# RWKV block with a routed mixture of experts: two tile lists in place of one, one gap tile a chunk, and the loads of x issued together

## The reference

```python
x = _ln(x, ln0_w, ln0_b)
h = _ln(x, ln1_w, ln1_b)
xx = _time_shift(h)
# xk, xv, xr: h and xx mixed; k, v, sr from three 128x128 matrices
att = _wkv(w, time_first, k, v)          # a scan along each sequence, with a running maximum
x = x + jnp.einsum('btc,oc->bto', sr * att, Wo)
# h2 = _ln(x); kf = relu(Wfk mix)^2; kv = Wfv kf; x + sigmoid(Wfr mix) * kv, then a layernorm
ys = _geglu(xf @ Ws1 + bs1) @ Ws2 + bs2                  # shared expert, all rows
top_val, top_idx = jax.lax.top_k(logits, 2)              # 2 of 12 experts a row
h = jnp.einsum('nd,edh->enh', xf, We1) + be1[:, None, :] # 128 -> 2 * 384, act 384 -> 128
yr = jnp.einsum('end,ne->nd', yE, w)
# layernorm(x + ys + yr)
```

## Time and profile before

| | |
|---|---|
| median of 3 runs | 449.29 us (448.38 to 449.96) |
| the profiled execution | 447.86 us |
| its span, first to last instruction | 446.1 us |
| busy in the span | PE 87%, DVE 70%, ACT 66%, POOL 57% |
| mean granted TensorE clock | 0.967 of full speed |

### The profile page before, as it was taken

The page is one execution under the profiler, slowest core; times in us unless marked ns, Lnnn a source line. Parts: engine busy times, 40 slices in busy tenths (PEclk is TensorE's granted clock), DMA queues, the critical chain, the costliest instruction groups (busy, mean ns, idle before and its releaser), DMA issues.

```text
span 446.1 us, 9927 instructions
## 1 busy us (share of the span) xinstructions
PE 388.3 (87%) x2503; PEld 304.1 (68%) x2503; DVE 311.9 (70%) x1065; ACT 296.4 (66%) x715; POOL 255.8 (57%) x328
## 2 busy tenths in 40 slices
PE   0466799999888997899999599999999999999991
PEld 0224456766665664657444399999999999999840
DVE  3899989999998999763774156666666656665162
ACT  2585689988978775586512177777777777777055
POOL 5676647586647877788777034444444444444273
PEclk9978889999999999999999699999999999999997
DMA  5289910000000300111134577677777677762484
GB/s 156 76 186 314 336 32 0 1 1 2 0 2 31 103 33 7 45 39 44 51 95 160 167 251 248 239 268 251 251 259 251 244 254 253 253 226 103 139 327 119
DMA packets 47247, 64.86 MB, mean 145 GB/s; under 512 B 8796, under 2 KB 31068, under 8 KB 47192
## 3 DMA queue, kind: packets, MB, share of 16 engines
q1 hardware_dynamic: 42744, 54.85, 36.6%
q0 software_dynamic: 4448, 9.38, 6.3%
HBM read 21.65 MB, written 13.91 MB: 80 GB/s over the span
## 4 chain that ended last, share of the span: by engine, by line
PE 57%; DVE 16%; POOL 12%; issue 7%; ACT 5%; DMA 2%; ACTq 0%; DVEq 0%; SPq 0%; POOLq 0%
PE bank L1279 23%; PE bank L1297 11%; POOL dispatched_rows L402 7%; PE bank L986 5%; PE bank L968 3%; DVE rec L554 3%; PE bank L919 2%; PE bank L1271 2%; DVE bst L474 2%; PE bank L920 2%; POOL frs L820 2%; ACT z L689 2%; PE bank L997 2%; PE bank L1330 2%; PE bank L998 2%
## 5 line engine op out<-in xcount | busy, mean ns | idle before, releaser
L1140 POOL DMA_INDIRECT routed_rows<-yo,goes_to x75 | 71.8, 957 | 98.7 <-DVE yo L1189 96.2
L1279 PE MATMUL bank<-xT,w 128*128 128x128 f32 x900 | 114.5, 277 | 0.3 <-issue 0.2
L1279 PEld LDWEIGHTS bank<-xT,w 128*128 128x128 f32 x900 | 108.0, 194 | 0.9 <-issue 0.9
L1181 DVE SCALAR_TENSOR_TENSOR actT<-bank,tile_bias,gl 128x128 f32<-128x128 f32 x225 | 65.2, 345 | 28.0 <-PE bank L1279 22.2
L1233 ACT ACTIVATE gl<-bank,tile_bias 128x128 f32<-128x128 f32 x225 | 66.2, 364 | 14.1 <-PE bank L1279 13.9
L402 POOL DMA_INDIRECT dispatched_rows<-rows_all,slot_i x64 | 64.0, 1000 | 18.6 <-issue 17.4
L1297 PE MATMUL bank<-we_sb,actT 128*128 x450 | 62.7, 275 | 0.9 <-DVE yo L1189 0.9
L1297 PEld LDWEIGHTS bank<-we_sb,actT 128*128 128x128 f32 x450 | 56.1, 192 | 1.2 <-issue 1.1
L1189 DVE SCALAR_TENSOR_TENSOR yo<-bank,goes,wb 128x128 f32<-128x128 f32 x75 | 26.3, 351 | 34.6 <-PE bank L1297 30.0
L1227 ACT ACTIVATE xT<-bank 128x128 f32<-128x128 f32 x75 | 20.8, 277 | 32.2 <-PE bank L1271 31.8
L968 PE MATMUL bank<-xk,wfk_sb 128*128 128x512 f32 x64 | 32.9, 624 | 5.0 <-DVE xk L571 4.5
(11 more groups left out here) (199 smaller groups left out, 761.7 us busy)
## 6 DMA issues: line engine op xcount, KB each, us to landing
w<-we_sb SPq DMA_DIRECT2D x75, 384.0 KB, 3.0
x_all<-dispatched_rows SPq DMA_DIRECT2D x75, 68.0 KB, 1.9
we_sb<-we SPq DMA_DIRECT2D x1, 4608.0 KB
...
routed_rows<-yo,goes_to POOLq DMA_INDIRECT x75
dispatched_rows<-rows_all,slot_i POOLq DMA_INDIRECT x64
```

The lines of the kernel that those rows point to most:

```text
L1140: ng.indirect_dma_start(routed, bass.IndirectOffsetOnAxis(ap=goes_to[n // U % DB][:, n % U:n % U + 1], axis=0), yo[n % YO][:, :], None).th ...
L1181: nv.scalar_tensor_tensor(actT[n % UA][:, at], ps_a[j][:, 0:P], tile_bias[:, j, n:n + 1], gl[n % 2][:, at], ALU.add, ALU.mult).then_inc(s2 ...
L1279: return nt.matmul(to[:, 0:P], w1[m][:, off:off + P], xT[m][:, :], start=True, stop=True)
```

## The change

Four parts.

1. The tile list is made twice. After batch 2 (48 of the 64 dispatches) `find_tiles(0)` lists 35 tiles (`AHEAD`) that are full whatever batch 3 brings; after batch 3 `find_tiles(1)` lists the other 40. Each list is told by one PE step `tell` of nine matmuls (words, owners, codes and biases together), into the bank pf1, and taken out by DVE alone. SP loads the first rows after 48 dispatches, and waits for the last 16, for the second list and for the pads only ahead of tile 35.
2. The pads are placed later: 7 by SP after the first ten row loads, 5 by ACT between its `shared_gelu` steps. The first two turns of x and two of the six gate matmuls of tile 0 stand on PE ahead of `shared_back(7)`.
3. `gaps` writes one tile `lead` (maximum less key) in place of two, and `below` makes four Relu instructions of [128 x 512] from it with per-channel biases.
4. All loads of x are issued without waits between them, three of them ahead of three weights. `number_rows` and the statistics of the first layernorm stand earlier on DVE, and POOL's `deviation0` takes chunks 2 to 7 in pairs.

```diff
+    FIRST_NORMS = ((0, 1), (1, 2), (2, 4), (4, 6), (6, 8))
+    LATE = BATCH[-1][0] * CT * K
+    AHEAD = -(-(LATE * P - E * (P - 1)) // P) // U * U
+    LISTS = ((0, AHEAD), (AHEAD, TILES))
+    SP_PADS = 7
...
+            load_x(0)
             sp.dma_start(rows_sb[:, :], rows.partition_broadcast(P)).then_inc(s["rows_loaded"], 16)
+            load_x(1)
             sp.dma_start(v_sb[:, :], vecs).then_inc(s["w_loaded"], 16)
             sp.dma_start(sq_sb[:, :, :], sqw.rearrange("s p c -> p s c")).then_inc(s["w_loaded"], 16)
+            load_x(2)
+            load_x(3)
             sp.dma_start(wfk_sb[:, :], wfk).then_inc(s["w_loaded"], 16)
             sp.dma_start(wfv_sb[:, :, :], wfv.rearrange("(j p) c -> p j c", p=P)).then_inc(s["w_loaded"], 16)
             sp.dma_start(wrt_sb[:, :], wrt).then_inc(s["w_loaded"], 16)
-            with sp.Fori(1, CH) as c:
-                sp.wait_ge(s["x_loaded"], c * 16)
-                sp.dma_start(x_all[:, ds(c * CT, CT), :], x_v[:, ds(c * CT, CT), :]).then_inc(s["x_loaded"], 16)
+            for c in range(4, CH):
+                load_x(c)
...
-                nv.scalar_tensor_tensor(by_sequence(gap[:, 0, :]), pp[:, :, 0:T], dec[:, 0:1], by_sequence(pk[:, :]),
-                                        ALU.add, ALU.subtract)
-
-                nv.scalar_tensor_tensor(by_sequence(gap[:, 1, :]), by_sequence(pk[:, :]), col(FIRST), pp[:, :, 0:T],
-                                        ALU.add, ALU.subtract).then_inc(s["delta_ready"], 1)
+                nv.tensor_tensor(by_sequence(lead[:, :]), pp[:, :, 0:T], by_sequence(pk[:, :]), ALU.subtract).then_inc(s["delta_ready"], 1)
...
-                na.activation(below_p[:, :, :], gap[:, :, :], ACT.Relu, scale=-1.0)
-                na.activation(below_m[:, :, :], gap[:, :, :], ACT.Relu).then_inc(s["gaps_ready"], 1)
+                na.activation(below_p[:, 0, :], lead[:, :], ACT.Relu, bias=dec[:, 5:6], scale=-1.0)
+                na.activation(below_m[:, 0, :], lead[:, :], ACT.Relu, bias=dec[:, 0:1])
+                na.activation(below_p[:, 1, :], lead[:, :], ACT.Relu, bias=dec[:, 9:10])
+                na.activation(below_m[:, 1, :], lead[:, :], ACT.Relu, bias=col(FIRST), scale=-1.0).then_inc(s["gaps_ready"], 1)
...
-            stats0(0); turn_rows(); stats0(1); stats1(0); prepare(); stats0(2); stats0(3); stats1(1); maximum(0); gaps(0)
-            number_rows(); stats0(4); stats1(2); weigh_v(0); states(0); carried(0); maximum(1); gaps(1); one_over(0); output(0)
+            stats0(0); turn_rows(); number_rows(); stats0(1); stats0(2); stats0(3); stats1(0); prepare(); stats0(4); stats1(1); stats0(5); maximum(0); gaps(0)
+            stats0(6); stats1(2); weigh_v(0); states(0); carried(0); maximum(1); gaps(1); one_over(0); output(0)
...
-            shared_act(1, 0); placed(v, 2, pT[:, PT_PREFIX]); x3(7); shared_act(1, 1); stats3(7)
-            shared_take(0); logits(6); shared_act(2, 0); shared_act(2, 1); logits(7); chosen(v, 3)
+            shared_act(1, 0); placed(v, 2, pT[:, PT_PREFIX]); find_tiles(0); leave_tiles(); x3(7); shared_act(1, 1); stats3(7)
+            shared_take(0); logits(6); shared_act(2, 0); shared_act(2, 1); tell_tiles(0); logits(7); chosen(v, 3)
             shared_take(1); shared_act(3, 0); shared_act(3, 1); placed(v, 3, pT[:, PT_PREFIX])
-            find_tiles(); shared_act(4, 0); shared_act(4, 1); shared_take(2); tell_tiles(); shared_take(3); shared_act(5, 0)
-            shared_act(5, 1); shared_take(4); shared_act(6, 0); shared_act(6, 1); shared_take(5)
+            count_pads(); shared_act(4, 0); shared_act(4, 1); shared_take(2); shared_take(3); find_tiles(1); shared_act(5, 0)
+            shared_act(5, 1); shared_take(4); shared_act(6, 0); shared_act(6, 1); shared_take(5); tell_tiles(1)
...
+            def place_pad(n):
+                if n == SP_PADS:
+                    a.wait_ge(s2["rows_known"], 1)
+                to = a.value_load(pad_at[0:1, n:n + 1], min_val=0, max_val=E * REGION - P)
+                na.dma_start(dispatch[ds(to, P), :], pad_rows[n * P:(n + 1) * P, :]).then_inc(s2["pads_placed"], 16)
+
+            def first_take(n):
+                a.wait_ge(s2["xT_psum"], n + 1)
+                na.activation(xT[n][:, :], pf0[:, 0:P], ACT.Copy).then_inc(s2["xT_ready"], 1)
...
+            shared_gelu(4, 0); shared_gelu(4, 1); place_pad(7); shared_gelu(5, 0); place_pad(8)
+            shared_gelu(5, 1); place_pad(9); shared_gelu(6, 0); place_pad(10); shared_gelu(6, 1); place_pad(11)
+            shared_gelu(7, 0); first_take(0); shared_gelu(7, 1)
...
-            deviation(0, "0"); weigh0(0); shift0(0); deviation(1, "0"); deviation(0, "1"); weigh0(1)
-            deviation(2, "0"); shift0(1); deviation(1, "1"); deviation(3, "0"); weigh0(2); shift0(2)
+            deviation0(0); deviation0(1); weigh0(0); shift0(0); weigh0(1); deviation(0, "1")
+            shift0(1); deviation0(2); deviation(1, "1"); weigh0(2); shift0(2)
...
+            def tell(late):
+                lo, hi = LISTS[late]
+                n = hi - lo
+                t.wait_ge(s2["code_ready"], late + 1)
                 t.wait_ge(s["relu_done"], CH * HF)
...
+                after2(t, "bias_ready", late)
+                nt.matmul(ps_tell[0:1, 0:n], word_at[:, late:late + 1], of_expert[:, lo:hi], start=True, stop=True)
+                nt.matmul(ps_tell[0:1, n:2 * n], low_p[0:EX, 0:1], of_expert[:, lo:hi], start=True, stop=True)
+                nt.matmul(ps_tell[:, 2 * n:3 * n], code_b[:, :], of_expert[:, lo:hi], start=True, stop=True)
                 for j in range(H1 // P):
-                    last = nt.matmul(ps_pre[:, j * TILES:(j + 1) * TILES], be1_sb[:, j * P:(j + 1) * P], of_expert[0:E, :],
+                    last = nt.matmul(ps_tell[:, (3 + j) * n:(4 + j) * n], be1_sb[:, j * P:(j + 1) * P], of_expert[0:E, lo:hi],
                                      start=True, stop=True)
                 last.then_inc(s2["bias_psum"], 1)
...
-            shared_up(1, 1); turn3(6); shared_gate(2, 0); router(6); shared_gate(2, 1); shared_up(2, 0)
+            shared_up(1, 1); turn3(6); shared_gate(2, 0); router(6); shared_gate(2, 1); shared_up(2, 0); tell(0)
...
-            shared_back(5); shared_up(6, 0); shared_gate(7, 0); shared_up(6, 1); shared_gate(7, 1)
-            shared_up(7, 0); shared_back(6); shared_up(7, 1); tell_biases(); shared_back(7)
+            shared_back(5); shared_up(6, 0); shared_gate(7, 0); shared_up(6, 1); tell(1); shared_gate(7, 1)
+            shared_up(7, 0); shared_back(6); first_turn(0); shared_up(7, 1); first_turn(1); first_gates(); shared_back(7)
...
-            sp.wait_ge(s["dispatched"], SLOTS // P * 16)
-            sp.wait_ge(s2["pads_placed"], E * 16)
+            sp.wait_ge(s["dispatched"], LATE * 16)
...
+                if n == 2 * U:
+                    for pad in range(SP_PADS):
+                        place_pad(pad)
                 if n >= 2 * U:
                     load_weights(n - U, owners.pop(n - U))
+                if n == AHEAD:
+                    sp.wait_ge(s2["tiles_known"], 2)
+                    sp.wait_ge(s["dispatched_late"], (SLOTS // P - LATE) * 16)
+                    sp.wait_ge(s2["pads_placed"], E * 16)
```

More of the change, by code:

```diff
@@ L261, in build @@
             s2[n] = sem("e_" + n)
+        x_loaded = [sem(f"x_loaded{c}") for c in range(CH)]
         x_loaded2 = [sem(f"x_loaded2_{m}") for m in range(XB)]
@@ L687, in apply @@
                     else:
-                        bias, scale = both[n][:, t, 0:1], both[n][:, t, 1:2]
+                        bias, scale = both[n][:, first + t, 0:1], both[n][:, first + t, 1:2]
                     last = na.activation(to[:, t, :], of[:, t, :], ACT.Identity, bias=bias, scale=scale)
```

248 lines of the change are left out of this document (139 added, 109 removed).

## The result

The changed kernel takes 444.7 us (median, 444.2 to 445.7) where the kernel before takes 449.4 (448.4 to 450.0): ratio 0.9901, 95% interval 0.9875 to 0.9927, so 4.7 us less. The prediction was 442.7, with a range of 438.0 to 447.0.

What follows compares the result with a forecast made beforehand. The prediction took TensorE to bound the routed experts, TensorE and VectorE together the attention part, with TensorE idle at the turn. Turn 3.6 plus attention 3.0 plus start 0 gave 6.6: 449.3 - 6.6 = 442.7 us, range 438.0 to 447.0.

Steps and rivals of the forecast that it cites:

- Predicted cost ahead of `shared_back(7)` 4.0: Shared part: lists, first turns and gates make the last back step end 4.0 us later, at 251.0.
- the wait at `prefix(3)`: Shared part: TensorE waits 1.3 us there because `tell_tiles(0)` puts VectorE 1.7 later against a slack of 0.3.
- The 0.9 for two turns and two gates: Ahead of `shared_back(7)`: four small f32 matmuls on TensorE at 0.22 us each, 0.9 later.
- the sum had 3.6: Turn: second matmuls of tile 0 start at 254.2 against 257.76, so the tile lists win 3.6 us.
- The rival that the lists take the place of the dispatch: Shared part: list waits cost 1.7 to 3.6 more and the attention gain fails: no change, 448.5; chance 0.09.
- I take half of that idle, 3.0: Attention part: 7.0 us less VectorE work saves half of TensorE's 6 us of VectorE-made idle, 3.0.
- VectorE alone: Attention part, rival: VectorE alone bounds it, all 7.0 us of relief count, 10.6 won in all: 438.7; chance 0.17.
- the ScalarE rival: Attention part: four longer Relus set the pace, 0.65 a chunk, 5.2 in eight chunks: 450.9; chance 0.09.
- I take 0: Start: TensorE's first matmul at 18.1 instead of 16.03 costs nothing by 42 us; bounds +2.1 and -0.5.
- the statistics' relief: Attention part: two calls of `stats0` leave VectorE's busy stretch for the start, 1.8 of its 7.0 us of relief.
- the forecast's own range: Whole kernel: 440.5 to 444.7 around the forecast of 442.7, given a chance of 0.42.
- the rival that TensorE bounds the attention part: Attention part: VectorE's relief stays unused, only the turn's 3.6 us are won: 445.7; chance 0.23.

Runs made afterwards that it cites:

- `after_again`: The changed kernel run again with no edit, in the first series of experiments: 443.94 us, ratio 0.9899 to the kernel before.
- turn-as-before run: `few_sems` with SyncE waiting for all dispatches and pads before row loads, first turns and gates behind the last back step, lists kept: 446.77 us, 0.9950; earlier on changed kernel 0.9942.
- `old_start`: The changed kernel with part 4 undone (loads of x, statistics, `number_rows` and POOL's order as before): 443.25 us, ratio 0.9884 to the kernel before.
- `few_old_start`: `few_sems` with part 4 undone: 443.71 us by the median of five, 443.12 without the execution of 1033.91; ratio without it 0.9861.
- `few_sems`: The changed kernel with 16 semaphores fewer, thresholds raised to match, no wait added or taken away: 443.40 us, ratio 0.9880 to the kernel before.
- `lists_only`: The changed kernel with parts 3 and 4 both undone, leaving lists, pads and first turns: 445.06 us, ratio 0.9923 to the kernel before.
- `old_gaps`: The changed kernel with part 3 undone (VectorE writes two differences a chunk, two Relus of 128x1024): 445.64 us, ratio 0.9947 to the kernel before.

## Why the prediction was right, and where its sizes were off

**The turn and the lists: right, step by step.** Predicted cost ahead of `shared_back(7)` 4.0, measured 3.87; it was to end at 251.0, and in `after_again` it starts at 248.76 and is 1.98 long. The single terms were off and cancel: `tell(0)` 1.9 for 2.3, the wait at `prefix(3)` 0.55 for 1.3, `shared_back(3)` at +3.0 relative to `mixed_channels(7)` for 4.0 (221.72 and 225.69), then `shared_back(4)` at +2.1 as predicted (228.73 before, 231.85 after). The 0.9 for two turns and two gates took a row of 0.45 as two records, where it is one; most of what they take lies in a wait of TensorE for VectorE, 0.84 long without them, so the misreading cost nothing. From the end of the back step to tile 0's second matmuls 3.2 predicted, 2.8 measured. So tile 0 gains 4.2 where the sum had 3.6. TensorE waits for no rows, weights or pads, the clock stays up, a tile takes 2.12. The rival that the lists take the place of the dispatch is out: they do take its place in part, as the turn-as-before run shows, but the earlier rows, with the earlier turns and gates, give another 3.1 to 3.4.

**The end: 1.3 us that the sum did not have.** In the profiles of all kernels with the lists the span ends 6.2 us behind ScalarE's last instruction, 4.9 before. The last store is not the cause: the DMA engines move its data until about 2.0 us behind that instruction in both (443.2 before, 439.7 in the first profile after). Then no engine and no DMA works for 2.9 us before and for 4.2 after, so the 1.3 lie behind all of the kernel's work. The last tile is 4.55 earlier in `after_again` (410.06 for 414.61), its execution 3.3 shorter (444.56 for 447.86). This is why parts 1 and 2 give 3.0 to 3.4 and not 4.2. Neither ScalarE's DMA queue nor the number of semaphores is the cause. It stays open; of the kernel before there is one profile, so that its end was the unusual one isn't excluded, nor is the length of the program tested.

**VectorE's relief: the size for `gaps` holds, where it is won is open.** The step was "I take half of that idle, 3.0", 2.2 of it for `gaps` and 0.8 for the statistics. Undoing part 3 cost 1.7 and 1.8 by the medians, so the first size holds (1.8 to 2.1 by the ratios). TensorE alone doesn't bound the attention part (its rival gave 0), nor VectorE alone (5.2). Taking VectorE's 0.7 a chunk away again, with ScalarE's Relus left as changed, cost 2.2, so ScalarE's extra (28.34 less 25.75 is 2.59 for the four, against 2.02 for the two, 24.62 to 26.64 before, +0.57 where I had 0.65) may cost 0.4 in eight chunks, or 0.9 by the ratios. That is a difference of two differences with scatter as large; the ScalarE rival, 5.2, is out. Both runs that load VectorE again also hand `lead` or `gap` to ScalarE 0.7 later, so whether the gain is VectorE's free time or the earlier hand-over is not tested. The Trainium skill, ScalarE: Activation LUTs, "Rules for kernel authors", sends relu and add to VectorE, with a speed per element in bf16 as its reason; here all is f32 and VectorE is the fuller engine, and moving its work to ScalarE's biases won 1.7 to 1.8 us.

**The start: the step that failed.** "I take 0" for the later start, and +0.8 for the statistics' relief. In its place the runs show a net cost. Three pairs that differ in part 4 alone went the same way by the ratios: 0.9899 and 0.9884, 0.9947 and 0.9923, 0.9880 and 0.9861. That is 0.2%, 0.9 us; the medians differ by 0.7, 0.6 and 0.3 (the last without the execution of 1033.91). So part 4 costs 0.3 to 0.9 us where the sum had a gain of 0.8. No pair alone tells the cost from nothing, and the three together do so barely; that the gain of 0.8 did not come is the firmer half. The chain was predicted well (weights 11.6, seen 11.31; first matmul 18.1, seen 17.89; `weigh_v` 30.1, seen 30.37), but that 42 us looks alike (42.02 for 41.97) was taken as the end of it. The profile of `old_start` reaches that point at 41.13, `few_old_start` at 41.09 where `few_sems` has 41.32, but `lists_only` at 42.39 where `old_gaps` has 42.33. Whether the later start is carried on, by which wait, or the earlier statistics are simply worth nothing, is not shown: the falls of the clock move each profile by as much.

**Sum.** On one chip 3.0 + 1.8 - 0.6 = 4.2, measured 4.1, against 3.6 + 3.0 + 0 = 6.6. The 2.5 too few are +0.6 at the turn, -1.3 at the end, -0.4 for `gaps` and -1.4 for the start with its statistics. The measured 444.7 lies at the edge of the forecast's own range and 2.0 above the forecast, but only 1.0 below the 445.7 of the rival that TensorE bounds the attention part. The one number would have spoken for that rival; only the run with part 3 undone speaks against it. The wide range, not the sum, took in the end and the start.
